# First self-attention of a decoder: second-half weight splits from GpSimd to ScalarE and VectorE, an own scratch for the normalised rows, the value bank emptied ahead of the inner norm's low parts, the decay prepared later

## Chip, core and metric

The kernel runs on one core of a Trainium2 chip. The metric is the device time in microseconds of one execution, the lower the better.

## The reference

Two decoder layers on x of 16 x 100 x 256, all in fp32. The change touches the first part only, layer 0's self-attention, which is a gated linear recurrence with a feed-forward part behind it:

```python
x = x + _L0_attn_ref(_layernorm(x), ...)      # then xattn, ffn, L1 attn, L1 xattn, L1 ffn

def _L0_attn_ref(x, ...):                     # B=16, L=100, 256 wide, H=16 heads of 64
    y = _layernorm(x) * ln1_g + ln1_b
    q, k, v = y @ Wq + bq, y @ Wk + bk, y @ Wv + bv      # each 256 -> 1024
    g = sigmoid(y @ Wg + bg)
    decay = sigmoid(decay_logit)[None, :, None]
    state = decay * state + k_t * v_t         # over the 100 steps
    out_t = g_t * q_t * state * DH ** -0.5
    x2 = x + out @ Wo + bo
    h = _layernorm(x2) * ln2_g + ln2_b
    return x2 + gelu(h @ W1 + b1) @ W2 + b2   # 256 -> 1024 -> 256
```

## The kernel before

The five engines have hand-written programs and wait for each other by counting semaphores; every order is the order of the code. An engine takes its instructions strictly in turn, so a wait holds all that stands behind it.

Rows go in 4 groups (NG) of 4 batch rows, 400 columns (N). The 1024 channels go in 8 blocks (KC) of 128. Block n of the whole stage is block n % 8 of group n // 8. TensorE's `project(n, kinds)` forms the four projections of a block, key, gate, value, query, each into a PSUM bank of its own (K_BANK0, G_BANK0, V_BANK0, Q_BANK0): only one block fits at a time, so a projection waits until the bank of the block before is emptied. ScalarE empties key and gate (`keys_gates`, into `kv` and `gate0`). VectorE empties value and query by multiplying them in (`gated`), and runs the recurrence (`scanned`: four scans and a product, into `state`). GpSimd splits the state (`heads_split`, into `oh0` and `ol0`), and TensorE sums it through Wo (`heads_summed`).

Each fp32 product is three matmuls on a high and a low part (fp32r): high is a cast, low the fp32 value less high. `split_matmul` (lines 764 to 766) does the three; the suffixes h and l name the parts (wk0h, wk0l, yTh, yTl, hTh, hTl, oh0, ol0; eh0 and el0 are the parts of the hidden values). The splits of weights and values are spread over ScalarE (casts), VectorE (`weights_low`) and GpSimd (`split`, lines 618 and 620). Before, the first column halves of Wk, Wg, Wv and Wq are split on ScalarE and VectorE, the second halves on GpSimd; Wo, W1 and W2 on ScalarE and VectorE.

At a group's end the steps are, on TensorE: the next group's first blocks (KC and KC+1, then keys and gates of KC+2) between the last head products, then the transposes of the inner norm's rows (`u0`, line 745), then value and query of KC+2, then `hidden` and `hidden_summed` (the feed-forward part). ScalarE writes the inner norm's rows to `full` and hTh, VectorE hTl from both, and both low parts (hTl of k = 0 and 1) are needed by the first hidden product. GpSimd's `hidden_split` splits the gelu's output from `full` into `eh0` and `el0`. Beside this VectorE rounds weights of a later layer (`blocks_rounded`, lines 2013 to 2019), and side jobs on TensorE transpose such weights; their results are parked in DRAM through the tile `parking`, which lies under `full`, `eh0` and `el0` in SBUF. Semaphore park_out counts these DMAs.

SP's queue loads x by groups and the weights, in the order of the code. ScalarE's queue loads the short vectors first, as rows of one tile, which TensorE turns into columns (`vec`, semaphore prep_vec; prep_done when ScalarE has copied them out).

## Time and profile before

| what | value |
|---|---|
| time, median of 3 runs | 1466.62 us (1465.25 to 1466.91) |
| the profiled execution: its own time | 1470.03 us |
| its span in the profile | 1468.2 us |
| granted TensorE clock over the span | 0.942 of full |
| TensorE busy | 1277.8 us, 87% |
| VectorE, ScalarE, GpSimd busy | 1043.7, 737.6, 256.4 us |

The table is read so: the span is from the first to the last instruction of one execution. The stage that is changed fills about the first 370 us of it. Busy times of engines overlap. A granted clock of 1 is 2.4 GHz, of 0.5 is 1.2 GHz.

### The profile page before, as it was taken

What the parts mean: (1) busy time and instruction counts of PE and PEld (TensorE: products, weight loads), DVE (VectorE), ACT (ScalarE), POOL (GpSimd) and SP (SyncE); (2) the same over time, 40 slices, a digit from 0 to 9 for tenths busy, and PEclk for the clock granted to TensorE, in tenths of its full rate; (3) what the DMA queues carried; (4) which work ended last, traced back from release to release, by engine and by line L of the source; (5) the groups of instructions that cost most, each with busy time, mean ns of one, the idle gap of its engine ahead of it and who ended that gap; (6) DMA issues with size and microseconds to landing.
All of it is one profiled execution on the core that took longest, in us unless ns stands there. A gap on an engine that the chain in (4) does not pass through costs nothing.

```text
span 1468.2 us, 27745 instructions
## 1 busy us (share of the span) xinstructions
PE 1277.8 (87%) x9826; PEld 1087.1 (74%) x9826; DVE 1043.7 (71%) x2592; ACT 737.6 (50%) x1808; POOL 256.4 (17%) x314
## 2 busy tenths in 40 slices
PE   4889888797899999999999999999879978969319
PEld 4878788796777777877778787877667756759318
DVE  5866466745567777777777777777589967885974
ACT  4442423325465555555655555565446643436473
POOL 3325252525100000000000000000044421000100
PEclk9899999998999999999999999999799989989759
DMA  9000101022100000000000000000020022300001
GB/s 282 31 22 1 44 1 44 1 77 80 35 11 11 12 1 11 10 11 10 11 11 10 1 10 11 10 1 1 1 58 2 3 66 62 100 7 1 0 0 46
DMA packets 34547, 40.66 MB, mean 28 GB/s; under 512 B 4889, under 2 KB 29066, under 8 KB 34442
## 3 DMA queue, kind: packets, MB, share of 16 engines
q1 hardware_dynamic: 33614, 39.24, 8.8%
q8 instruction: 51, 0.84, 0.2%
q14 instruction: 54, 0.44, 0.1%
q10 hardware_dynamic: 828, 0.14, 0.1%
HBM read 35.36 MB, written 4.01 MB: 27 GB/s over the span
## 4 chain that ended last, share of the span: by engine, by line
PE 51%; DVE 16%; issue 5%; ACT 4%; POOL 1%; DVEq 0%; ACTq 0%; POOLq 0%
PE bank L764 8%; PE bank L766 7%; PE bank L765 7%; PE bank L975 4%; PE bank L959 4%; PE bank L967 3%; PE bank L935 3%; ACT prob L1634 2%; DVE amax L2454 2%; DVE nmx L2270 2%; PE bank L1208 1%; PE bank L1226 1%; DVE kTl L2048 1%; PE bank L996 1%; PE bank L1293 1%
## 5 line engine op out<-in xcount | busy, mean ns | idle before, releaser
L1634 ACT ACTIVATE prob<-bank,nmx 100x361 f32<-100x361 f32 x256 | 142.7, 560 | 156.6 <-DVE nmx L2270 155.7
L2270 DVE TENSOR_REDUCE nmx<-bank 100x1 f32<-100x361 f32 x256 | 124.2, 526 | 22.8 <-PE bank L959 15.7
L690 POOL TENSOR_TENSOR frstd<-fmoments,eps 100x1 f32<-100x1 f32 x32 | 6.2, 193 | 648.5 <-DVE fmoments L2213 648.4
L764 PE MATMUL bank<-cxTh,wxkh 128*128 128x362 f32 x256 | 99.9, 390 | 2.8 <-DVE kTl L2048 2.8
L975 PEld LDWEIGHTS bank<-pT,vv 128*64 128x64 f32 (+1 forms) x1536 | 71.2, 139 | 37.5 <-issue 28.2
L975 PE MATMUL bank<-pT,vv 128*64 128x100 f32 (+1 forms) x1536 | 96.6, 261 | 1.9 <-DVE oTl L2047 1.8
L2287 DVE TENSOR_SCALAR prob<-prob,rsum 100x361 f32<-100x361 f32 x256 | 92.9, 405 | 4.5
L967 PE MATMUL bank<-ident,prob 100*128 100x100 f32 (+1 forms) x768 | 90.7, 254 | 1.5 <-DVE prob L2287 1.5
L967 PEld LDWEIGHTS bank<-ident,prob 100*128 100x128 f32 (+1 forms) x768 | 85.5, 153 | 7.1 <-DVE prob L2287 2.6
L2047 DVE TENSOR_TENSOR oTl<-bank,oTh 128x100 fp32r<-128x100 f32 x128 | 32.9, 257 | 81.2 <-ACT oTh L1620 78.0
L1620 ACT CAST oTh<-bank 128x100 fp32r<-128x100 f32 x128 | 31.8, 249 | 112.6 <-PE bank L975 112.4
L764 PE MATMUL bank<-wxvh,cxTh 128*128 128x512 f32 (+1 forms) x192 | 84.4, 440 | 2.8 <-DVE vv L2194 2.8
L765 PE MATMUL bank<-cxTl,wxkh 128*128 128x362 f32 x256 | 83.9, 328 | 0.0
L766 PE MATMUL bank<-cxTh,wxkl 128*128 128x362 f32 x256 | 83.9, 328 | 0.0
L2048 DVE SCALAR_TENSOR_TENSOR kTl<-bank,vec,kTh 128x362 fp32r<-128x362 f32 x128 | 75.2, 588 | 12.0 <-ACT kTh L1603 11.8
L1603 ACT ACTIVATE kTh<-bank,vec 128x362 fp32r<-128x362 f32 x128 | 72.3, 565 | 20.6 <-PE bank L766 20.2
L766 PE MATMUL bank<-wxvh,cxTl 128*128 128x512 f32 (+1 forms) x192 | 76.1, 396 | 0.0
L1985 DVE SCALAR_TENSOR_TENSOR kv<-bank,vec,kv 128x400 f32<-128x400 f32 x32 | 20.2, 632 | 78.1 <-PE bank L766 78.0
L765 PE MATMUL bank<-wxvl,cxTh 128*128 128x512 f32 (+1 forms) x192 | 75.4, 393 | 0.0
L935 PE MATMUL bank<-zT,wxq 128*128 (+1 forms) x256 | 58.9, 353 | 8.4 <-DVE oTl L2047 7.9
L715 POOL TENSOR_TENSOR s<-s,mx 100x400 f32<-100x400 f32 x64 | 54.2, 857 | 63.0 <-DVE mx L2349 61.2
L1626 ACT COPY pT<-bank 128x400 f32<-128x400 f32 x128 | 63.7, 498 | 1.6 <-PE bank L967 1.6
(403 smaller groups left out, 3794.8 us busy)
## 6 DMA issues: line engine op xcount, KB each, us to landing
cx<-in_ctx_dram SPq DMA_DIRECT2D x32, 128.0 KB, 2.1
xc<-in_ctx_dram SPq DMA_DIRECT2D x32, 128.0 KB
parked_weights<-parking SPq DMA_DIRECT2D x9, 256.0 KB, 5.6
mask_i<-in_mask_BxS_ik_dram SPq DMA_DIRECT2D x16, 141.0 KB
w<-in_L_attn_W_dram SPq DMA_DIRECT2D x2, 1024.0 KB, 13.6
cx<-in_ctx_dram SPq DMA_DIRECT2D x16, 105.0 KB, 2.1
xc<-in_ctx_dram SPq DMA_DIRECT2D x16, 105.0 KB
x<-in_x_dram SPq DMA_DIRECT2D x4, 400.0 KB
```

Source lines behind the costliest of these rows:

```text
L764: pe.matmul(o, wh, mh, start=start, stop=False)
L765: pe.matmul(o, wh, ml, start=False, stop=False)
L766: return pe.matmul(o, wl, mh, start=False, stop=stop)
L935: mm = pe.matmul(o[:, 0:2 * T], wxq[:, k, c * P:(c + 1) * P], zT[:, ds(pair_of_rows, 1), k, :].rearrange("d a q -> d (a q)"), start=(k == ...
L967: mm = pe.transpose(bank[T_BANKS[kt // 2]][0:r, col:col + T], prob[:, (2 * c + e) % 4, k0:k0 + r], ident[0:T, 0:T])
L975: mm = pe.matmul(bank[O_BANK][e * DH:(e + 1) * DH, 0:T], vv[0:r, kt, c * P + e * DH:c * P + (e + 1) * DH], pT[0:r, c % 2, kt, e * T:(e + 1 ...
L1603: nc.scalar.activation(kTh[:, c, :], src[:, 0:SP], ACT.Identity, bias=column("L0_xattn_bk", c)).then_inc(xa_kh, 1)
L1626: nc.scalar.copy(pT[:, c % 2, 0:2, :], bank[T_BANKS[0]][:, 0:4 * T].rearrange("p (k q) -> p k q", k=2))
L1634: nc.scalar.activation(prob[:, h % 4, :], bank[S_BANKS[e]][0:T, 0:S], ACT.Exp, bias=nmx[:, h:h + 1], accum_out=psum_[:, h:h + 1]).then_inc ...
L2048: return nc.vector.scalar_tensor_tensor(dst, src, bias, high.bitcast(F32), ALU.add, ALU.subtract)
L2270: nc.vector.tensor_reduce(nmx[:, h:h + 1], bank[S_BANKS[e]][0:T, 0:S], AX_X, ALU.max, negate=True).then_inc(xa_max, 1)
L2287: nc.vector.tensor_scalar(prob[:, h % 4, :], prob[:, h % 4, :], rsum[:, h:h + 1], None, ALU.mult).then_inc(xa_p, 1)
```

## The change

- The second halves of Wk, Wg, Wv and Wq are no longer split on GpSimd: ScalarE casts them in group 0 (keys and gates after block 1, values and queries after block 2), and VectorE takes the low parts behind block 1 and block 2. For that, statistics of x groups 1 to 3 move one block later on VectorE.
- SP loads Wo and the second halves ahead of the x groups 1 to 3.
- ScalarE writes the normalised rows to a new tile `y_rows`, not to `full`. So `rows_high0` no longer waits for hidden splits or for parking; the wait for parking now stands before the attention sums of groups 1 to 3.
- The decay's sigmoid goes behind the first weight casts, its transpose behind block 0 on TensorE, its copy behind block 0's key and gate on ScalarE; VectorE's first `gated` waits for it. The vectors are copied behind the first group's square roots.
- At a group's end VectorE empties and scans block KC+1 before hTl, and waits for GpSimd's first hidden split (l0_es) before the long additions and roundings.

```diff
@@ sync (SP)
                 load_half(name, dst, 0, wa_in[n])
+            load_raw("L0_attn_Wo", wo0[:], wo_in)
+            for name, dst in projections:
+                load_half(name, dst, 1, wb_in)
             for g in range(1, NG):
                 load_rows(g)
-            for name, dst in projections:
-                load_half(name, dst, 1, wb_in)
-            load_raw("L0_attn_Wo", wo0[:], wo_in)
@@ gpsimd
-                    nc.gpsimd.tensor_tensor(yTl[:, k, :], full[:, k, :], yTh[:, k, :].bitcast(F32), ALU.subtract).then_inc(l0_z, 1)
+                    nc.gpsimd.tensor_tensor(yTl[:, k, :], y_rows[:, k, :], yTh[:, k, :].bitcast(F32), ALU.subtract).then_inc(l0_z, 1)
             rows_low0(0)
-            pool.wait_ge(wb_in, 64)
-            for high, low, w in ((wk0h, wk0l, wk0), (wg0h, wg0l, wg0), (wv0h, wv0l, wv0), (wq0h, wq0l, wq0)):
-                split(high[:, :, 512:], low[:, :, 512:], w[:, :, 512:], l0_wb)
@@ tensor
-            pe.transpose(bank[SIDE_BANK0][:, 0:NV], rows[:], ident[0:NV, 0:NV])
-            pe.wait_ge(prep_decay, 1)
-            pe.transpose(bank[SIDE_BANK0][:, NV:NV + KC], decay_rows[:].rearrange("c h d -> c (h d)"), ident[0:KC, 0:KC])\
-                .then_inc(prep_vec, 1)
+            pe.transpose(bank[SIDE_BANK0][:, 0:NV], rows[:], ident[0:NV, 0:NV]).then_inc(prep_vec, 1)
...
                 project(c, range(4))
+                if c == 0:
+                    pe.wait_ge(prep_decay, 1)
+                    pe.transpose(bank[SIDE_BANK0][:, 0:KC], decay_rows[:].rearrange("c h d -> c (h d)"), ident[0:KC, 0:KC])\
+                        .then_inc(prep_vec, 1)
@@ scalar, rows_high0 and sums_out
-                if g:
-                    act.wait_ge(l0_es, KC * (g - 1))
-                if g > 1:
-                    act.wait_ge(park_out, 16 * 3 * (g - 1))
...
-                elif g == NG - 1:
+                elif g:
                     act.wait_ge(park_out, 16 * 3 * g)
@@ scalar, group 0
             first_deviations(1, 0, 1)
+            act.wait_ge(prep_vec, 1)
+            nc.scalar.mul(vecs[:], bank[SIDE_BANK0][:, 0:NV], DH ** -0.5)
+            nc.scalar.copy(vec[:], bank[SIDE_BANK0][:, 0:NV]).then_inc(prep_done, 1)
...
                     keys_gates(0)
+                    act.wait_ge(prep_vec, 2)
+                    nc.scalar.copy(decay[:], bank[SIDE_BANK0][:, 0:KC]).then_inc(prep_done, 1)
                     weights_high(wo_in, 16, wo0h, wo0, slice(0, D))
                     keys_gates(1)
+                    weights_high(wb_in, 64, wk0h, wk0, slice(512, C))
+                    weights_high(wb_in, 64, wg0h, wg0, slice(512, C))
                 for c in range(2, KC):
                     if c > 2 or g == 0:
                         keys_gates(first + c)
+                    if g == 0 and c == 2:
+                        weights_high(wb_in, 64, wv0h, wv0, slice(512, C))
+                        weights_high(wb_in, 64, wq0h, wq0, slice(512, C))
@@ vector, group 0
-            dve.wait_ge(prep_done, 1)
+            dve.wait_ge(prep_done, 2)
...
                 if g == 0:
-                    first_stats(1)
                     gated(0)
                     scanned(0)
                     weights_low(4, wo0l, wo0, wo0h, slice(0, D))
                     gated(1)
                     scanned(1)
+                    weights_low(5, wk0l, wk0, wk0h, slice(512, C), l0_wb)
+                    weights_low(6, wg0l, wg0, wg0h, slice(512, C), l0_wb)
...
                         if c == 2:
+                            weights_low(7, wv0l, wv0, wv0h, slice(512, C), l0_wb)
+                            weights_low(8, wq0l, wq0, wq0h, slice(512, C), l0_wb)
+                            first_stats(1)
+                        if c == 3:
                             first_stats(2)
-                        if c == 3:
                             first_stats(3)
@@ vector, group end
+                if follows:
+                    gated(first + KC + 1)
+                    scanned(first + KC + 1)
                 for k in range(KD):
                     dve.wait_ge(l0_hh, KD * g + k + 1)
                     nc.vector.tensor_tensor(hTl[:, k, :], full[:, k, :], hTh[:, k, :].bitcast(F32), ALU.subtract).then_inc(l0_h, 1)
                 if follows:
-                    gated(first + KC + 1)
-                    scanned(first + KC + 1)
                     gated(first + KC + 2)
                     scanned(first + KC + 2)
+                    dve.wait_ge(l0_es, first + 1)
```

VectorE in group 0, from block 1's value and query on. Names are tiles, `kv<-bank` empties the value bank. Before:

```order
L1985 SCALAR_TENSOR_TENSOR kv<-bank,vec,kv 128x400
L1989 SCALAR_TENSOR_TENSOR gate<-bank,vec,gate 128x400
L2000 SCALAR_TENSOR_TENSOR state<-decay,kv 128x100 x4
L2004 SCALAR_TENSOR_TENSOR state<-gate,state 128x400
L1985 SCALAR_TENSOR_TENSOR kv<-bank,vec,kv 128x400
L1989 SCALAR_TENSOR_TENSOR gate<-bank,vec,gate 128x400
L2000 SCALAR_TENSOR_TENSOR state<-decay,kv 128x100 x4
L2004 SCALAR_TENSOR_TENSOR state<-gate,state 128x400
L1931 MEMSET pause 1x1
L1933 BN_STATS stats_all<-x 100x6 x4
```

And now:

```order
L1987 SCALAR_TENSOR_TENSOR kv<-bank,vec,kv 128x400
L1991 SCALAR_TENSOR_TENSOR gate<-bank,vec,gate 128x400
L2002 SCALAR_TENSOR_TENSOR state<-decay,kv 128x100 x4
L2006 SCALAR_TENSOR_TENSOR state<-gate,state 128x400
L1980 TENSOR_TENSOR wk0l<-wk,wk0h 128x2x512
L1980 TENSOR_TENSOR wg0l<-wg,wg0h 128x2x512
L1987 SCALAR_TENSOR_TENSOR kv<-bank,vec,kv 128x400
L1991 SCALAR_TENSOR_TENSOR gate<-bank,vec,gate 128x400
L2002 SCALAR_TENSOR_TENSOR state<-decay,kv 128x100 x4
L2006 SCALAR_TENSOR_TENSOR state<-gate,state 128x400
L1980 TENSOR_TENSOR wv0l<-wv,wv0h 128x2x512
L1980 TENSOR_TENSOR wq0l<-wq,wq0h 128x2x512
```

Four low parts have come in (L1980), two behind block 1 and two behind block 2, and the statistics of x (BN_STATS) stand behind them. What GpSimd had there (its rows now begin with oh) is gone from its queue.

VectorE at the first group's end, from the inner norm's rows on. Before:

```order
L1864 TENSOR_SCALAR u<-zg,moments,rstd 100x256 x4
L2150 TENSOR_TENSOR hTl<-full,hTh 128x400 x2
L1985 SCALAR_TENSOR_TENSOR kv<-bank,vec,kv 128x400
L1989 SCALAR_TENSOR_TENSOR gate<-bank,vec,gate 128x400
L2000 SCALAR_TENSOR_TENSOR state<-decay,kv 128x100 x4
L2004 SCALAR_TENSOR_TENSOR state<-gate,state 128x400
L1985 SCALAR_TENSOR_TENSOR kv<-bank,vec,kv 128x400
L1989 SCALAR_TENSOR_TENSOR gate<-bank,vec,gate 128x400
L2000 SCALAR_TENSOR_TENSOR state<-decay,kv 128x100 x4
L2004 SCALAR_TENSOR_TENSOR state<-gate,state 128x400
L2157 TENSOR_TENSOR x<-x,zg 100x1024
```

And now:

```order
L1866 TENSOR_SCALAR u<-zg,moments,rstd 100x256 x4
L1987 SCALAR_TENSOR_TENSOR kv<-bank,vec,kv 128x400
L1991 SCALAR_TENSOR_TENSOR gate<-bank,vec,gate 128x400
L2002 SCALAR_TENSOR_TENSOR state<-decay,kv 128x100 x4
L2006 SCALAR_TENSOR_TENSOR state<-gate,state 128x400
L2159 TENSOR_TENSOR hTl<-full,hTh 128x400 x2
L1987 SCALAR_TENSOR_TENSOR kv<-bank,vec,kv 128x400
L1991 SCALAR_TENSOR_TENSOR gate<-bank,vec,gate 128x400
L2002 SCALAR_TENSOR_TENSOR state<-decay,kv 128x100 x4
L2006 SCALAR_TENSOR_TENSOR state<-gate,state 128x400
L2165 TENSOR_TENSOR x<-x,zg 100x1024
```

One block's value, query and scans (kv to state) have moved ahead of the low parts hTl. The addition to x (last row) now waits for GpSimd's first hidden split.

ScalarE from the square roots to block 1's key. Before:

```order
L1434 ACT_TABLE_LOAD
L1434 ACTIVATE decay_rows<-logits 8x128
L1437 COPY decay<-bank 128x8
L1438 ACTIVATE vecs<-bank 128x80
L1439 COPY vec<-bank 128x80
L1455 ACT_TABLE_LOAD
L1455 ACTIVATE std_all<-first_moments,eps 100x4
L1457 ACTIVATE std_all<-var_z,eps 100x4
L1512 CAST wk0h<-wk 128x2x512
L1512 CAST wg0h<-wg 128x2x512
L1468 ACTIVATE full<-bank,vec 128x400
L1469 ACTIVATE yTh<-bank,vec 128x400
```

And now:

```order
L1449 ACT_TABLE_LOAD
L1449 ACTIVATE std_all<-first_moments,eps 100x4
L1451 ACTIVATE std_all<-var_z,eps 100x4
L1511 ACTIVATE vecs<-bank 128x80
L1512 COPY vec<-bank 128x80
L1502 CAST wk0h<-wk 128x2x512
L1502 CAST wg0h<-wg 128x2x512
L1458 ACTIVATE y_rows<-bank,vec 128x400
L1459 ACTIVATE yTh<-bank,vec 128x400
L1458 ACTIVATE y_rows<-bank,vec 128x400
L1459 ACTIVATE yTh<-bank,vec 128x400
L1502 CAST wv0h<-wv 128x2x512
```

The sigmoid of the decay and its table load are gone from the head, and y_rows takes the place of full.

## Rows read from the trace of the kernel before

**Rows 1.** The page, busy times of the engines.

```profile
PE 1277.8 (87%) x9826; PEld 1087.1 (74%) x9826; DVE 1043.7 (71%) x2592; ACT 737.6 (50%) x1808; POOL 256.4 (17%) x314
```

**Rows 2.** TensorE's waits, 0 to 450 us: total, times, longest.

```profile
PE bank L764 <- DVE kv L1985: 20.0, 5, 7.2
PE bank L764 <- POOL yTl L639: 11.7, 4, 3.9
...
PE bank L764 <- POOL el L620: 10.7, 16, 1.7
```

**Rows 3.** Windows after six waits: busy of five engines, granted clock (0.50), DMA, GB/s.

```profile
42.22:47.38 5.16, 5.16 (x15) 5.16 (x16) 3.76 (x9) 0.00 (x0) 2.45 (x3) 0.50 0.01 3
101.76:105.40 3.64, 3.64 (x11) 3.60 (x12) 2.74 (x7) 0.10 (x1) 1.35 (x2) 0.53 0.00 0
164.07:170.24 6.17, 6.17 (x18) 6.11 (x19) 0.00 (x0) 1.78 (x3) 1.45 (x2) 0.50 0.00 0
184.95:190.78 5.83, 5.83 (x18) 5.78 (x19) 4.09 (x12) 0.09 (x1) 1.56 (x2) 0.50 0.00 0
248.55:252.20 3.65, 3.65 (x11) 3.61 (x12) 0.00 (x0) 0.59 (x1) 1.44 (x2) 0.53 0.00 0
268.19:272.69 4.50, 4.50 (x13) 4.46 (x14) 2.76 (x8) 0.10 (x1) 1.56 (x2) 0.50 0.00 0
```

**Rows 4.** Timelines of ScalarE and TensorE, the start: start, length, instruction.

```profile
8.83 1.28 ACT L1434 ACT_TABLE_LOAD   x1 [8.83 <-issue]
...
13.55 0.30 ACT L1455 ACTIVATE std_all<-first_moments,eps 100x4 f32<-100x4 f32 x1
...
21.26 0.70 PE L764 MATMUL bank<-yTh,wk0h 128*128 128x400 f32 x1 [2.95 <-POOL yTl L639]
```

**Rows 5.** Timeline of VectorE, group 0.

```profile
29.12 6.90 DVE L2000 TENSOR_TENSOR_SCAN state<-decay,kv 128x100 f32<-128x100 f32 x4
...
37.20 4.42 DVE L1978 TENSOR_TENSOR wo0l<-wo,wo0h 128x2048 fp32r<-128x2048 f32 x1
...
53.90 1.12 DVE L2000 TENSOR_TENSOR_SCAN state<-decay,kv 128x100 f32<-128x100 f32 x4
...
57.83 2.25 DVE L1978 TENSOR_TENSOR w1l<-w,w1h 128x2048 fp32r<-128x2048 f32 x1
```

**Rows 6.** Timeline of GpSimd, first and last of its second-half splits (8 instructions).

```profile
25.31 1.04 POOL L618 CAST wk0h<-wk 128x1024 fp32r<-128x1024 f32 x1 [4.10 <-DMA wq<-in_L_attn_Wq_dram]
...
36.93 2.55 POOL L620 TENSOR_TENSOR wq0l<-wq,wq0h 128x1024 fp32r<-128x1024 f32 x1
```

**Rows 7.** Timelines: TensorE and ScalarE, rows of groups 1 and 2.

```profile
83.65 0.45 PE L764 MATMUL bank<-yTh,wk0h 128*128 128x400 f32 x1 [1.29 <-POOL yTl L639]
...
160.51 0.68 ACT L1468 ACTIVATE full<-bank,vec 128x400 f32<-128x400 f32 x1 [4.73 <-DMA parked_weights<-parking]
```

**Rows 8.** SP's timeline and the DMA list (last column: us to landing).

```profile
22.36 3.98 SPq L509 DMA_DIRECT2D raw<-in_L_attn_W_attn_dram  x1
...
raw<-in_L_attn_W_attn_dram SPq DMA_DIRECT2D x1, 768.0 KB, 13.5
```

**Rows 9.** Timelines at the first group's end: VectorE, TensorE, GpSimd.

```profile
100.59 0.57 DVE L2150 TENSOR_TENSOR hTl<-full,hTh 128x400 fp32r<-128x400 f32 x1 [0.57 <-ACT hTh L1566]
...
131.27 0.63 DVE L1985 SCALAR_TENSOR_TENSOR kv<-bank,vec,kv 128x400 f32<-128x400 f32 x1 [8.83 <-PE bank L766]
...
101.76 0.51 PE L764 MATMUL bank<-yTh,wv0h 128*128 128x400 f32 x1 [4.05 <-DVE kv L1985]
...
108.62 1.88 POOL L620 TENSOR_TENSOR el<-full,eh 128x400 fp32r<-128x400 f32 x1
...
120.91 2.42 POOL L620 TENSOR_TENSOR el<-full,eh 128x400 fp32r<-128x400 f32 x1
...
123.87 1.05 POOL L620 TENSOR_TENSOR el<-full,eh 128x400 fp32r<-128x400 f32 x1
```

More of the change, by code:

```diff
@@ L205, in decoder_kernel @@
             el0 = sb("el0", [P, 2, N], F32R, scope=s)
+            y_rows = sb("y_rows", [P, KD, N], scope=s)
         with ExitStack() as s:
@@ L771, in side_job @@
                 o = bank[SIDE_BANK0 + j % 2]
+                if j == 0:
+                    pe.wait_ge(prep_done, 2)
                 if raw is not None:
@@ L1431, in _ @@
             act.dma_start(rel[0:BUCKETS, :], a["L1_attn_rel_emb"]).then_inc(small_in, 16)
-            act.wait_ge(vec_in, 16 * VEC_DMAS)
-            nc.scalar.activation(decay_rows[:], logits[:].unsqueeze(2).broadcast_to([KC, 2, DH]), ACT.Sigmoid)\
-                .then_inc(prep_decay, 1)
-            act.wait_ge(prep_vec, 1)
-            nc.scalar.copy(decay[:], bank[SIDE_BANK0][:, NV:NV + KC])
-            nc.scalar.mul(vecs[:], bank[SIDE_BANK0][:, 0:NV], DH ** -0.5)
-            nc.scalar.copy(vec[:], bank[SIDE_BANK0][:, 0:NV]).then_inc(prep_done, 1)
             act.wait_ge(memsets, 2)
@@ L1467, in rows_high0 @@
                     src, scale, bias = bank[SIDE_BANK0 + k][:, 0:N], column("L0_attn_ln1_g", k), column("L0_attn_ln1_b", k)
-                    nc.scalar.activation(full[:, k, :], src, ACT.Identity, scale=scale, bias=bias)
+                    nc.scalar.activation(y_rows[:, k, :], src, ACT.Identity, scale=scale, bias=bias)
                     nc.scalar.activation(yTh[:, k, :], src, ACT.Identity, scale=scale, bias=bias).then_inc(l0_y, 1)
@@ L1524, in _ @@
             weights_high(wa_in[3], 16, wq0h, wq0, slice(0, 512))
+            nc.scalar.activation(decay_rows[:], logits[:].unsqueeze(2).broadcast_to([KC, 2, DH]), ACT.Sigmoid)\
+                .then_inc(prep_decay, 1)
             for g in range(NG):
@@ L1973, in rows_once_normalized, with weights_low @@
                 link(ins)
-            def weights_low(n, low, w, high, cols):
+            def weights_low(n, low, w, high, cols, done=l0_wl):
                 dve.wait_ge(l0_wh, n + 1)
-                nc.vector.tensor_tensor(low[:, :, cols], w[:, :, cols], high[:, :, cols].bitcast(F32), ALU.subtract).then_inc(l0_wl, 1)
+                nc.vector.tensor_tensor(low[:, :, cols], w[:, :, cols], high[:, :, cols].bitcast(F32), ALU.subtract).then_inc(done, 1)
             def gated(n):
@@ L2108, in _ @@
                         if c == 2:
+                            weights_low(7, wv0l, wv0, wv0h, slice(512, C), l0_wb)
+                            weights_low(8, wq0l, wq0, wq0h, slice(512, C), l0_wb)
+                            first_stats(1)
+                        if c == 3:
                             first_stats(2)
-                        if c == 3:
                             first_stats(3)
                             first_variances(1, NG)
-                            weights_low(5, w1l, w1, w1h, slice(0, C))
+                            weights_low(9, w1l, w1, w1h, slice(0, C))
                         if c == 4:
                             second_variances(3, 1, NG)
-                            weights_low(6, w2l, w2, w2h, slice(0, D))
+                            weights_low(10, w2l, w2, w2h, slice(0, D))
                             both_deviations(3, 1, NG)
```

## Prediction

> **What bounds the kernel now.** I read the page's first part, then the list of TensorE's waits, then the timelines of the engines around each long wait. TensorE is busy 87% of the span [rows 1]; it is the engine to keep fed. Over the first 450 us, where all edits lie, its list of waits has three lines that this change can touch [rows 2]: 20.0 us for the value bank (line 1985 on VectorE empties it), 11.7 us for the low parts of the rows (yTl), 10.7 us for the low parts of the hidden values (el). Nothing after about 370 us is edited, so what is saved before should arrive at the end unchanged: nothing there runs at a fixed time.
>
> A wait costs more than its length. After the six longest waits the granted clock is 0.50 to 0.53, that is 1.2 instead of 2.4 GHz, for 3.6 to 6.2 us each [rows 3]; at full clock the same matmuls need about half, so each window costs half its length: 2.6, 1.8, 3.1, 2.9, 1.8 and 2.3 us. A wait of 1.29 [rows 7] and those for el, none longer than 1.7 [rows 2], have no such window behind them.
>
> **The change part by part.**
>
> Head start. ScalarE begins with the sigmoid's table at 8.83 and only reaches the square root at 13.55; TensorE's first projection starts at 21.26, behind a chain of root, rows, transposes and splits [rows 4]. With the sigmoid gone, the table loaded at 8.83 is the root's, so the root starts at 8.83+1.28 = 10.11 and the whole chain 3.4 us earlier: **3.4 us**. The copies of the vectors go behind the two roots and end near 12, before the rows are ready (13.3).
>
> Stall in the first group. GpSimd splits the second halves from 25.31 to 39.5 (36.93+2.55) [rows 6]. Beside it VectorE's four scans take 6.90 us where 1.12 is usual, and the split of Wo 4.42 where one of the same size takes 2.25 [rows 5]. So the value bank of the second column block (block 1) is emptied only when TensorE has waited 7.2 us for it, until 42.22 [rows 2, 3]. With those splits off GpSimd, VectorE comes to that block 5.8+2.2 = 8 us earlier. Wait 7.2 and slow window 2.6 go: **9.8 us**.
>
> What it costs there. VectorE gets four subtractions, each half of the 2.25 one [rows 5]: some 4.6 us; ScalarE gets four casts, which I put at 1 us each (GpSimd's took 1.04 [rows 6]). I laid the engines out. At half clock a matmul takes 5.16/15 = 0.34 [rows 3], at full clock then 0.17 to 0.18, and the four projections of a block (24 matmuls) 4.3; block 0 starts at 17.8, mostly at half clock, and ends near 24.8. ScalarE: decay copy 25.4, Wo's cast to 27.3, then the halves at 28.5 and 32.2. VectorE must wait for the decay (25.4 instead of 24.0) and behind the scan and Wo's low part empties block 1's value bank near 32, needed at 31.6 (wait 0.5); the raw weights for the first side transposes land at 22.36+13.5 = 35.9 [rows 8], which nothing in the change hastens, while TensorE is there at 35.4 (0.5); the statistics of groups 2 and 3 and W1's low parts now stand behind a VectorE that is already late, so block 4's value bank is emptied near 54.8 against 51.9 needed (2.9). Three losses of 1 us on VectorE beside GpSimd's splits of the state are in this. Without them the wait of 2.9 is nearly gone; with whole splits (1.6 us) lost instead, it is about 5. I take **-4** in all, bounds -1 and -6.5.
>
> A rule speaks here. Beside GpSimd's work the scans, which read decay and kv from SBUF, took six times their usual time, and Wo's low part twice [rows 5]. So who comes second may lose a whole instruction of the other. "SBUF — State Buffer" of the Trainium skill (Who interferes with whom) says that a VectorE instruction with two SBUF inputs and a GpSimd one that reads SBUF exclude each other for the whole instruction. The trace agrees for these two. By that rule the moved subtractions, with two such inputs, would lose whole instructions too: the -4 would then be -6.5 and the time 1433.
>
> Rows' own scratch. Before groups 2 and 3 ScalarE waits for the parking DMAs (4.73 us, until 160.51) because `full` lies under them [rows 7]. With y_rows it doesn't. In group 1's turn, which has no such wait, TensorE still waits 1.29 [rows 7]. So the waits before groups 2 and 3, which are the rest of the 11.7 after 2.95 and 1.29 [rows 2, 4, 7], 7.4 together, become 1.3 each: 4.8, and two windows (3.1+1.8) go: **9.7 us**. The wait for parking moves to the attention sums on ScalarE. Between the old wait's end and these stand the rows' evictions and low parts (3.5 us), two projections (2.2) and a head product (1.1), 6.8 us, and the rows now come 2.6 earlier: still 4 us behind the DMA. Landing 4 us later, it would be seen.
>
> Value bank before the low parts. At each of three boundaries TensorE waits 4.0 us for the value bank (4.05, 3.99, 3.99; the 20.0 less 7.2 and a small 0.7) [rows 2, 9]. VectorE is then idle till ScalarE's high parts are there. Its inputs (the next group's block 1: value and query) were projected before the keys and gates of block 2, which TensorE has just finished, so it empties the bank at 97.4; TensorE, free at 97.7, goes on at once. The scan ends at 99.6, before the second high part releases the low one (100.59, ends 101.2) [rows 9]. Then the value and query projections take 2.2 us, and the hidden product waits for the low parts: 101.2-99.9 = 1.3, and about 1.45 in the other two. Gain 12.0 - 4.2 = 7.8, and the windows 1.8+2.9+2.3 = 7.0 go: **14.8 us**. If VectorE's scan ran slowly there, only the 1.3 would grow.
>
> The new wait on the first hidden split. VectorE now starts its long additions and roundings after GpSimd's first el. Before, that subtraction took 1.88 where 1.05 is usual [rows 9], and TensorE's longest wait for el was 1.7 [rows 2]. Three times some 1.1 us: +3.2. But the roundings then begin about 2.5 us later against TensorE and meet the last splits, with no slack behind. Nothing before shows that order: bounds +3.2 and -5; I take **+2**. VectorE itself has 8.83 us idle behind the roundings [rows 9], so its lateness alone costs nothing.
>
> First statistics later and x loaded later: groups 1 to 3 of x are needed after 43 now, and are loaded ahead of W1 and of the raw weights, in by 35.9: nothing.
>
> **Sum.** 3.4+9.8-4+9.7+14.8+2 = 35.7 us. The profiled execution took 1470.03 around its span of 1468.2, so this one would take 1434.3 with a span of 1432.5; the median of the three runs is 1466.62, so 1430.9, say 1431. Own range, 1426 to 1437.
>
> **The rivals.**
> - *VectorE becomes the bound in group 0.* It works nearly without a pause from 25 to 60 already in my layout. If its low parts lose time beside GpSimd as Wo's did (2.2 us each), the bank waits grow by 4 to 6, and the wait of 2.9 becomes as long as those with a slow window behind: gain 29, 1437. 14%.
> - *The roundings lock out the last hidden splits.* The low part (line 620) took 2.42 instead of 1.05 where it met them before, at 120.91 [rows 9], in the sixth split, with two uncontended ones behind. If seventh and eighth meet them, each group loses 1.4+1.4, and the +2 becomes 3.2-8.4 = -5: gain 29, 1438. 9%.
> - *The wait only moves at the boundary.* If the low parts come 2 us later than I think, the wait before the hidden product is as long as those that have a slow window behind them now [rows 3]: 3 x (2+2): gain 24, 1443. 5%.
> - *Nearly none of the new waits.* The -4 is -1, the splits +3: gain 40, 1427 or a little less. 8%.
> - *Slower.* Wo and the second halves share one queue and ScalarE waits for all four halves with block 2's key eviction behind it. They landed at 25.3 [rows 6], are needed at 28.5; each us beyond is a us of TensorE. They would have to land after 28.5+36 = 64 to end slower. The raw weights behind them in the queue were in by 35.9 [rows 8], so 2%.
> The forecast itself: 62%.
>
> **Numbers.** 1424 to 1442 holds the forecast and the first two rivals whole, and leaves out the third, the slower one and a bit of the fourth; it is wide because the contention has no row for the new order. A difference within 0.2% (3 us) can't be told from none: no case lies there but a mishap, 1%; slower 2%; faster 97%.
>
> **What the profile after would show.** First projection near 17.8; no value wait of 7 us near 35, scans of 1.1 us throughout group 0; casts of second halves on ScalarE before 35; row evictions of groups 2 and 3 without a DMA wait; at the boundaries the value projection straight behind the transposes, and a wait of 1.3 to 1.5 for hTl at full clock; the first el at 1.05. Wrong would be: a long wait for kv in group 0 with the clock at half behind it, hTl after 102 (in old time), or el of splits 6 to 8 above 2 us in every group.

## The result and the profile after

The changed kernel takes 1442.83 us (median of 4 runs, 1441.94 to 1443.37), the kernel before beside it 1466.59 (1465.25 to 1466.91): ratio 0.984, 95% interval 0.9825 to 0.9854. It is 23.8 us faster; 35.7 were forecast, and 1442.83 lies just above the range of 1424 to 1442. The profiled execution took 1443.37 with a span of 1441.2, 27.0 less than before.

The page's busy times answer to [rows 1], TensorE's waits up to 450 us (total, times, longest) to [rows 2]:

```profile
PE 1271.4 (88%) x9826; PEld 1080.2 (75%) x9826; DVE 1044.2 (72%) x2596; ACT 740.2 (51%) x1811; POOL 249.8 (17%) x306
```

```profile
PE bank L759 <- DVE hTl L2159: 8.7, 4, 2.4
PE bank L759 <- POOL el L621: 8.7, 8, 2.3
PE bank L759 <- POOL yTl L640: 6.7, 4, 2.9
...
PE bank L759 <- DVE kv L1987: 1.4, 2, 0.7
PE bank L786 <- DMA raw<-in_L_attn_W_attn_dram: 1.0, 1, 1.0
```

The value bank's 20.0 us are down to 1.4, those for yTl from 11.7 to 6.7 as worked out. But hTl, 2.4 before (one wait, in the last group), stands at 8.7, and el has lost only 2.0 while its longest wait grew from 1.7 to 2.3. The windows behind the new waits (columns as in [rows 3]: stretch, length, busy of five engines, granted clock, DMA, GB/s):

```profile
92.01:95.14 3.13, 3.13 (x9) 3.10 (x10) 2.56 (x7) 0.59 (x1) 0.03 (x1) 0.50 0.00 0
112.02:115.50 3.48, 3.48 (x11) 3.43 (x12) 0.00 (x0) 0.00 (x0) 1.44 (x2) 0.55 0.02 5
187.08:190.50 3.42, 3.42 (x11) 3.37 (x12) 0.00 (x0) 0.00 (x0) 1.45 (x2) 0.56 0.02 5
244.06:248.00 3.94, 3.94 (x15) 3.92 (x16) 3.00 (x7) 1.19 (x2) 1.77 (x3) 0.68 0.00 0
167.87:171.00 3.13, 3.13 (x17) 3.13 (x18) 3.01 (x7) 1.19 (x2) 0.96 (x2) 1.00 0.00 0
```

The first four stretches have half clock in them: the first from its start, the next two from 0.4 us on (9 to 11 matmuls in 3.1 to 3.5 us), the fourth only from 1.4 us on (0.68 in the mean). The last one, at full clock, holds 17 matmuls in 3.13. By this count half clock costs about 1.5 us each time; priced as in the prediction, at half of the time spent at half clock, it is 1.7, the figure used below.

The chain at the start (ScalarE, TensorE; [rows 4]), then VectorE and GpSimd in the first group ([rows 5, 6]):

```profile
8.84 1.28 ACT L1449 ACT_TABLE_LOAD   x1 [8.84 <-issue]
10.14 0.30 ACT L1449 ACTIVATE std_all<-first_moments,eps 100x4 f32<-100x4 f32 x1
...
17.85 0.70 PE L759 MATMUL bank<-yTh,wk0h 128*128 128x400 f32 x1 [2.95 <-POOL yTl L640]
```

```profile
28.24 2.29 DVE L1980 TENSOR_TENSOR wo0l<-wo,wo0h 128x2048 fp32r<-128x2048 f32 x1
...
31.53 1.50 DVE L2002 TENSOR_TENSOR_SCAN state<-decay,kv 128x100 f32<-128x100 f32 x4
...
33.56 1.22 DVE L1980 TENSOR_TENSOR wk0l<-wk,wk0h 128x1024 fp32r<-128x1024 f32 x1
34.70 1.54 DVE L1980 TENSOR_TENSOR wg0l<-wg,wg0h 128x1024 fp32r<-128x1024 f32 x1
```

```profile
28.39 2.51 POOL L619 CAST oh<-state 128x400 fp32r<-128x400 f32 x1 [10.59 <-DVE state L2006]
```

The start gained 3.41 (3.4 forecast). Scans and low parts now run at or near their usual length. It is GpSimd's cast (usually 0.52) that takes 2.51 beside Wo's low part, and nobody waits for it.

The first group's end, VectorE, GpSimd and TensorE, which answers to [rows 9]:

```profile
87.73 1.13 DVE L2002 TENSOR_TENSOR_SCAN state<-decay,kv 128x100 f32<-128x100 f32 x4
88.89 0.57 DVE L2006 SCALAR_TENSOR_TENSOR state<-gate,state 128x400 f32<-128x400 f32 x1
89.38 0.57 DVE L2159 TENSOR_TENSOR hTl<-full,hTh 128x400 fp32r<-128x400 f32 x1
90.50 1.37 DVE L2159 TENSOR_TENSOR hTl<-full,hTh 128x400 fp32r<-128x400 f32 x1 [0.54 <-ACT hTh L1568]
```

```profile
89.53 0.80 POOL L619 CAST oh<-state 128x400 fp32r<-128x400 f32 x1 [6.12 <-DVE state L2006]
90.41 1.02 POOL L621 TENSOR_TENSOR ol<-state,oh 128x400 fp32r<-128x400 f32 x1
```

```profile
92.01 0.67 PE L759 MATMUL bank<-hTh,w1h 128*128 128x400 f32 x1 [2.12 <-DVE hTl L2159]
```

The state that VectorE now finishes at 89.5 releases GpSimd's split of it (oh, ol), and this split lies right on hTl: the second part, begun 0.09 behind ol, takes 1.37 where 0.57 is usual, and TensorE waits 2.12, not 1.3.

And the roundings, VectorE, GpSimd, TensorE:

```profile
96.78 1.51 DVE L2165 TENSOR_TENSOR x<-x,zg 100x1024 f32<-100x1024 f32 x1 [2.18 <-POOL el L621]
...
109.13 1.95 DVE L2021 TENSOR_TENSOR raw<-raw,blk_scale 128x1536 f32<-128x1536 f32 x1
```

```profile
95.71 1.05 POOL L621 TENSOR_TENSOR el<-full,eh 128x400 fp32r<-128x400 f32 x1
...
97.29 1.91 POOL L621 TENSOR_TENSOR el<-full,eh 128x400 fp32r<-128x400 f32 x1
...
109.55 2.42 POOL L621 TENSOR_TENSOR el<-full,eh 128x400 fp32r<-128x400 f32 x1
```

```profile
112.02 0.45 PE L759 MATMUL bank<-eh,w2h 128*128 128x400 f32 x1 [2.34 <-POOL el L621]
```

VectorE waits 2.18 us for the first el, which is 1.05 long now; the next one takes the 1.91 instead. The rounding's last multiplication begins at 109.13 and meets the seventh split, whose subtraction takes 2.42.

Checkpoints of TensorE in both profiles; a gain is the start before less the start after, a step is what a stage adds to it:

| start of | before | after | gain | step | forecast |
|---|---|---|---|---|---|
| first projection | 21.26 | 17.85 | 3.41 | 3.4 | 3.4 |
| projection of group 1 | 83.65 | 73.62 | 10.03 | 6.6 | 5.8 |
| hidden, group 0 | 105.60 | 92.01 | 13.59 | 3.6 | 4.55 |
| key of block 11 on ScalarE | 129.03 | 117.16 | 11.87 | -1.7 | +0.7 |
| projection of group 2 | 164.07 | 149.57 | 14.50 | 2.6 | 2.5 |
| hidden, group 1 | 189.12 | 167.87 | 21.25 | 6.75 | 8.55 |
| key of block 19 on ScalarE | 212.85 | 192.21 | 20.64 | -0.6 | +0.7 |
| projection of group 3 | 248.55 | 225.70 | 22.85 | 2.2 | 2.3 |
| hidden, group 2 | 272.36 | 244.06 | 28.30 | 5.45 | 6.65 |
| key of block 27 on ScalarE | 295.80 | 267.88 | 27.92 | -0.4 | +0.7 |
| end | 1468.2 | 1441.2 | 27.0 | -0.9 | 0 |

The forecast column is made of the prediction's terms, cut at these points. "Hidden" is the first hidden product of a group, so the half clock behind the wait for hTl counts in the step after it. The three boundaries (the steps up to "hidden") lack 4.0 us, the three hidden phases (the steps up to "key of block") 4.8, the end 0.9; the first group gave 0.8 more.

### The profile page after: what moved, and what is told of

It is laid out like the page before. It is cut to its first block, busy times and chain, and to the rows that moved or that the text cites. A ratio compares the mean times of both kernels' runs of the same rounds, so it can differ in the third digit from the quotient of the medians.

```text
span 1441.2 us, 27742 instructions
## 1 busy us (share of the span) xinstructions
PE 1271.4 (88%) x9826; PEld 1080.2 (75%) x9826; DVE 1044.2 (72%) x2596; ACT 740.2 (51%) x1811; POOL 249.8 (17%) x306
## 4 chain that ended last, share of the span: by engine, by line
PE 51%; DVE 17%; issue 5%; ACT 4%; POOL 1%; DVEq 0%; ACTq 0%; POOLq 0%
PE bank L759 8%; PE bank L761 7%; PE bank L760 7%; PE bank L976 4%; PE bank L960 4%; PE bank L968 3%; PE bank L936 3%; ACT prob L1636 2%; DVE amax L2462 2%; DVE nmx L2278 2%; PE bank L1209 1%; PE bank L1227 1%; DVE kTl L2050 1%; PE bank L997 1%; PE bank L1241 1%
## 5 line engine op out<-in xcount | busy, mean ns | idle before, releaser
L1605 ACT ACTIVATE kTh<-bank,vec 128x362 fp32r<-128x362 f32 x128 | 72.2, 564 | 20.9 <-PE bank L761 20.5
```

The lines of the kernel that those rows point to most:

```text
L1605: nc.scalar.activation(kTh[:, c, :], src[:, 0:SP], ACT.Identity, bias=column("L0_xattn_bk", c)).then_inc(xa_kh, 1)
```

## The experiments

The kernel before was timed again beside these kernels: 1467.54 us beside the first four below, 1468.54 beside c_both, c_both_no_wait, b_group0 and b_bank_first, 1468.03 beside the other four. So they are compared with the change by their ratios to it, and by their medians; a thousandth is 1.5 us, and the change stands at 0.984 (0.9825 to 0.9854).

**a_no_wait: the changed kernel without the new wait.**

```diff
                     scanned(first + KC + 2)
-                    dve.wait_ge(l0_es, first + 1)
```

> The changed kernel without VectorE's wait for GpSimd's first hidden split. Theory A (the wait shifts the roundings onto the seventh split): the roundings start 2.2 us earlier, the first el takes 1.9 instead of 1.05, the seventh 1.05 to 1.7 instead of 2.42; TensorE's waits for el stay under 1.8 and the half clock behind the seventh goes in the two groups that have it. Gain (1.3 + 1.7) x 2 + 0.5, less 0.9 x 3: about 4 us, 1439. Rival B (the wait brings what I had put on it, +2, and the loss lies elsewhere): 1445. Within 1 us of 1443 would say that both sides cancel.

Measured: 1443.32 us, ratio 0.9838 (0.9824 to 0.9852), no different from the change. In the first group the first two el are at 1.04 and 1.06, the last multiplication comes at 106.51 and falls on a cast, and no wait for el is above 0.7. In the second and third group it falls on a subtraction again (2.42 both times); the third:

```profile
259.37 1.95 DVE L2021 TENSOR_TENSOR raw<-raw,blk_scale 128x1536 f32<-128x1536 f32 x1
```

```profile
262.26 0.45 PE L759 MATMUL bank<-eh,w2h 128*128 128x400 f32 x1 [2.32 <-POOL el L621]
```

TensorE waits 8.5 us for el against 8.7, and half clock follows the wait of 2.32. So the new wait is worth nothing that can be told from noise: neither A nor B. Without it VectorE loses its time to the splits in other places; what decides is which split the last multiplication meets.

**a_lows_first: the old order at the boundary.**

```diff
-                if follows:
-                    gated(first + KC + 1)
-                    scanned(first + KC + 1)
                 for k in range(KD):
                     dve.wait_ge(l0_hh, KD * g + k + 1)
...
                 if follows:
+                    gated(first + KC + 1)
+                    scanned(first + KC + 1)
```

> The changed kernel with hTl ahead of the scan of block KC+1 again at each group end; all else as changed. Theory A: the order of the boundary brought most of what I forecast for it (14.8) less 0.8 x 3 of a slower hTl and some 3.4 of half clock: it costs 9 to 11 us to undo, 1452 to 1454, with waits of 4.0 for kv at three boundaries and half clock behind them. Rival B (the order brought nearly nothing, the slow hTl ate it): 1444 to 1447. Rival C (the full 14.8, the shortfall is elsewhere): 1458.

Measured: 1455.53 us, ratio 0.9917 (0.9899 to 0.9935): (0.9917 - 0.984) x 1467 = 11.3 us above the change by the ratios, with some 3.5 of uncertainty, and 12.7 by the medians. The waits for kv are back (12.8 in 4, longest 4.1), with half clock behind each of the three at the boundaries. That is A's 9 to 11 or a little more. C, the full 14.8, lies at the edge of that uncertainty.

**a_scan_split: the state's product behind hTl.**

```diff
                 if follows:
                     gated(first + KC + 1)
-                    scanned(first + KC + 1)
+                    scans(first + KC + 1)
                 for k in range(KD):
...
                 if follows:
+                    weighed(first + KC + 1)
                     gated(first + KC + 2)
```

(`scans` is the four scans, `weighed` the product with gate0.)

> The changed kernel with only the product with the gate (which lets GpSimd split the state) moved behind both hTl; the bank is emptied and the four scans run ahead of hTl as in the change. Theory A (GpSimd's split of that state slows the second hTl): hTl takes 0.57 instead of 1.37, TensorE's wait before the hidden product 1.3 instead of 2.1 in all three groups, and if a wait of 1.3 has no half clock behind it, two windows of 1.7 go too: 2.4 + 3.4 = 6 us, 1437. Without the windows 1440.5. Rival B (hTl is slow for another reason, ScalarE's reads of PSUM or the write to hTh beside it): hTl stays at 1.37 and the time at 1443.

Measured: 1442.80 us, ratio 0.9843 (0.9827 to 0.9858): no gain. The mechanism at the boundary is as A had it, VectorE, GpSimd, TensorE:

```profile
90.35 0.57 DVE L2168 TENSOR_TENSOR hTl<-full,hTh 128x400 fp32r<-128x400 f32 x1 [0.51 <-ACT hTh L1568]
```

```profile
91.47 0.52 POOL L619 CAST oh<-state 128x400 fp32r<-128x400 f32 x1 [8.19 <-DVE state L2010]
```

```profile
91.07 0.42 PE L759 MATMUL bank<-hTh,w1h 128*128 128x400 f32 x1 [1.38 <-DVE hTl L2168]
...
108.39 0.45 PE L759 MATMUL bank<-eh,w2h 128*128 128x400 f32 x1 [1.20 <-POOL el L621]
...
112.08 0.70 PE L759 MATMUL bank<-eh,w2h 128*128 128x400 f32 x1 [2.33 <-POOL el L621]
```

All six hTl take 0.57 to 0.58, the wait is 1.3 to 1.4 in all three groups, at full clock. That the split of the state was what slowed hTl is shown. But the roundings end when they did (109.19 + 1.95), so TensorE and the splits, a us earlier, meet them one split later: TensorE waits 1.20 more for the seventh split, and 2.33 with half clock for the eighth, on which the last multiplication now falls, in all three groups: el 12.8 us against 8.7. What the boundary gave, the roundings took. (The expectation for c_both below calls these the sixth and seventh split; counted in the trace they are the seventh and eighth.)

**a_round_late: the last multiplication behind the eighth split.**

```diff
                 link(nc.vector.tensor_scalar(flat, flat, 7.0, -8.0, ALU.min, ALU.max))
+                dve.wait_ge(l0_es, splits)
                 nc.vector.tensor_tensor(blocks(flat), blocks(flat), over(blk_scale[:], n), ALU.mult).then_inc(prep_q, 1)
```

(`splits` is first + KC, all of the group's hidden splits.)

> The changed kernel with the last multiplication of the block rounding (1.95 us, two operands from SBUF) held until the group's eighth hidden split is done. Theory A: el of the seventh split 1.05 instead of 2.42, TensorE's wait for it (2.34, 2.34, 1.74) falls by 1.3 each, and the half clock behind it in two groups (1.7 each) goes: 3.9 + 3.4 = 7 us, 1436. VectorE then ends near 115.6 and is next needed at 119.4, so its lateness costs nothing. Rival B (the seventh split is slow from the clock or from PSUM, or the next split takes the wait over): 1441 to 1443.

Measured: 1436.27 us, ratio 0.9786 (0.9769 to 0.9803), 6.6 us faster than the change by the medians, 7.9 by the ratios: A. GpSimd, VectorE, TensorE:

```profile
110.32 1.02 POOL L621 TENSOR_TENSOR el<-full,eh 128x400 fp32r<-128x400 f32 x1
```

```profile
113.04 1.76 DVE L2022 TENSOR_TENSOR raw<-raw,blk_scale 128x1536 f32<-128x1536 f32 x1 [3.17 <-POOL el L621]
117.69 0.63 DVE L1987 SCALAR_TENSOR_TENSOR kv<-bank,vec,kv 128x400 f32<-128x400 f32 x1 [2.89 <-PE bank L761]
```

```profile
111.40 0.45 PE L759 MATMUL bank<-eh,w2h 128*128 128x400 f32 x1 [0.94 <-POOL el L621]
```

The seventh split takes 1.02 instead of 2.42, the longest wait for el is 0.9 and no half clock stands behind one (in the first three groups only behind one wait for hTl, 2.07, and the one for the raw weights). VectorE still has 2.89 us idle behind it. This was so although this execution waited 3.24 us for the raw weights in group 0, with 1.7 of half clock, against 0.98 in the change's.

**The parts alone, on the kernel before.** Each diff is the matching piece of the change and nothing else.

*b_group0: head, second halves, loads, statistics and decay.*

> The kernel before with the first group's part of the change alone (head, second-half splits off GpSimd, order of loads, statistics, decay); rows in the old scratch, old order at the group ends, no new wait. By my terms 3.4 + 9.8 - 4 = 9.2 us off, 1457 to 1458; by the trace of the changed kernel 10.3, and 12 if the roundings and later windows fall well. Rival (part of the gain of the first group needs the other parts): 1460 or more.

Measured: 1459.70 us, ratio 0.9934 (0.9917 to 0.9951), 8.8 less than before beside it and 0.3 short of the rival's 1460; by the ratio it is 9.7. Group 1's projection starts at 73.56, as in the change (73.62), so this stage did not need the other parts.

*b_bank_first: value bank and scan ahead of hTl, without the new wait.*

> The kernel before with block KC+1's value bank emptied and scanned ahead of hTl, and nothing else. By my term 14.8 off: 1452. By the changed kernel's trace the slow hTl (0.8 x 3) and half clock behind hTl remain: 9 to 12 off, 1455 to 1458, as undoing it in the changed kernel cost 12.7. Rival (what it frees is taken back by the waits for the parked rows in groups 2 and 3 and by el): 1460 or more.

Measured: 1458.90 us, ratio 0.9929 (0.9910 to 0.9948), 9.6 less, far from my term of 14.8 and 0.9 above the 1455 to 1458 expected from the changed kernel's trace. Its hTl is slow too (1.34 at 98.85, wait 2.20 with half clock behind it), but its waits for el are no longer than 1.6. Its first group is the code of before, and there TensorE waited 5.67 for the value bank where before's profile has 7.24. From the first projection to that of group 1 it took 60.8 us (21.09 to 81.91), before's profiled execution 62.4 (21.26 to 83.65), and b_rows_only, with the same order in this group, 61.3 (22.71 to 83.98): before's was the slowest of the three, by 1.1 to 1.6 us.

*b_rows_only: y_rows.*

> The kernel before with the rows' own scratch alone. By my term 9.7 off: 1458. By the changed kernel's trace the two waits for the parked rows go to 1.3 (2.6 and 2.2 saved) with their half clock (3.1 and 1.8, of which the clock list shows 1.7 each): 8.2 off, 1459.5. Rival (part of it goes into the next long wait for kv, which stands right behind in both groups): 1462 or more.

Measured: 1460.02 us, ratio 0.9945 (0.9928 to 0.9962), 8.0 less. The waits for yTl in front of groups 2 and 3 fall to 1.25 and 1.23; the waits for kv that follow them are 3.99 and 4.05, as they were, so nothing of the gain went there.

The three gains add up to 28 us by the ratios, with some 4 to 5 of uncertainty, and to 26.4 by the medians, against 23.8 for the change. That they take from each other, because an earlier TensorE meets the same roundings, would fit a_scan_split, but the difference is not clear of the noise.

**c_both: both orders together** (a_scan_split and a_round_late).

> The changed kernel with both orders: the state's product behind hTl, and the last multiplication of the block rounding behind the eighth hidden split. Theory A (the product's order gave 0.8 us a boundary, which the last multiplication took back at the sixth and seventh split): against the order of the rounding alone (1436.3) it now keeps 2.3 us, and the half clock behind hTl that one group still had (1.7): 1432 to 1433. Rival B (what is gained at the boundary is always taken back by the multiplication in the middle, which isn't moved): 1435 to 1437.

Measured: 1436.80 us, ratio 0.9781 (0.9767 to 0.9795), as a_round_late alone. The time is B's, but not for B's reason: the multiplication in the middle did not take the gain back. TensorE waits 1.20 and 0.94 for el in each group, and still its trace keeps a gain for 200 us: at the last group's head sums (before 329.24) it is at 293.25, a_round_late at 295.70. Then it loses the 2.4 again: 8.5 us of clock go between 294 and 311 where a_round_late loses 6.8, and from the cross-attention's first product to the end it takes 1100.3 against 1099.2 us, in code that is the same.

**c_both_no_wait: the same without the new wait.**

> As the kernel with both orders, but also without VectorE's wait for the first hidden split. The additions and roundings start up to 2.5 us earlier, so the multiplication in the middle meets the fourth or fifth split and not the fifth or sixth. Theory A (the wait of the change is worth nothing, only moves which split is slow): within 1.5 us of the kernel with both, 1431 to 1434. Rival B (it is worth its +2): 1434.5 or more.

Measured: 1437.28 us, ratio 0.9787 (0.9774 to 0.9801). The time is in B's range only because c_both itself was 4 us above what A took for it; against c_both the difference is 0.5, so the new wait is worth nothing here that can be seen in the time. The traces differ more. Both have the same two waits for el, 1.2 and 0.94, close together in each group; behind them the clock stays full in c_both (first line) and falls in c_both_no_wait in two groups of three (second line):

```profile
111.92:115.60 3.68, 3.68 (x20) 3.68 (x21) 1.76 (x1) 1.19 (x2) 0.00 (x0) 1.00 0.00 0
110.68:114.00 3.32, 3.32 (x12) 3.32 (x11) 1.43 (x1) 0.00 (x0) 0.00 (x0) 0.50 0.00 0
```

In return its wait of 2.17 for the raw weights has no half clock behind it, where c_both's 2.93 has.

**a_eh_scalar: ScalarE writes the high part of the hidden values.**

```diff
-                split(eh0[:, n % 2, :], el0[:, n % 2, :], full[:, n % 2, :], l0_es)
+                nc.gpsimd.tensor_tensor(el0[:, n % 2, :], full[:, n % 2, :], eh0[:, n % 2, :].bitcast(F32), ALU.subtract)\
+                    .then_inc(l0_es, 1)
...
-                    nc.scalar.activation(full[:, c % 2, :], bank[SIDE_BANK0 + c % 2][:, 0:N], ACT.Gelu,
-                                         bias=column("L0_attn_b1", c)).then_inc(l0_gelu, 1)
+                    src = bank[SIDE_BANK0 + c % 2][:, 0:N]
+                    nc.scalar.activation(full[:, c % 2, :], src, ACT.Gelu, bias=column("L0_attn_b1", c))
+                    if n == 0:
+                        act.wait_ge(line_in, 16)
+                    if n > 1:
+                        act.wait_ge(l0_w2, KD * (n - 1))
+                    nc.scalar.activation(eh0[:, c % 2, :], src, ACT.Gelu, bias=column("L0_attn_b1", c)).then_inc(l0_gelu, 1)
```

> The changed kernel with the high part of the hidden values written by ScalarE (the same gelu once more, 0.59 us) and GpSimd left with the subtraction only: 1.05 to 2.4 a block where it has 1.6 to 3.7. Theory A (what TensorE waits for is GpSimd's row of splits, pushed by the roundings): waits for el nearly gone, 8.7 us to 2 or less, with the half clock behind the seventh split: some 6.5 + 3.4 = 10 us off, 1433; hTl is still slow. Rival B (TensorE's pace of 2.2 us a block is near ScalarE's now, and the second gelu delays the first split by 0.6): 1438 or more.

Measured: 1439.58 us, ratio 0.9808 (0.9793 to 0.9822), 3.3 us faster by the medians, 4.7 by the ratios, less than half of what A said. GpSimd now stands idle between the subtractions, but that does not help it past the multiplication:

```profile
106.43 1.05 POOL L635 TENSOR_TENSOR el<-full,eh 128x400 fp32r<-128x400 f32 x1 [0.75 <-ACT eh L1583]
108.59 2.39 POOL L635 TENSOR_TENSOR el<-full,eh 128x400 fp32r<-128x400 f32 x1 [1.10 <-ACT eh L1583]
```

It stands idle 1.10 us and is then held all the same by the multiplication at 108.34; TensorE waits 2.06 in two groups, with half clock behind both. So the row of splits was a part of the wait, and the single collision, which a_round_late takes away for 6.6 to 7.9, the larger one.

**c_raw: c_both, raw weights ahead of W1 and W2 in SP's queue.**

> The kernel with both orders, and the first raw weights (for TensorE's first side transposes) loaded ahead of W1 and W2. In the profile of the kernel with both orders TensorE waits 2.93 us for that DMA, with 1.7 of half clock behind it; in the changed kernel 0.98. Theory A: the wait goes in every execution: 1 to 4.6 us off, 1432 to 1435.5, and a narrower spread. Rival B (W1 and W2 land later and stop ScalarE's casts, or the value banks of group 0 wait in its place): 1436 or more.

Measured: 1437.55 us, ratio 0.9787 (0.9770 to 0.9805): no gain, B. The wait for the DMA is gone, and two blocks later TensorE waits for VectorE:

```profile
52.06 0.45 PE L759 MATMUL bank<-yTh,wv0h 128*128 128x400 f32 x1 [1.87 <-DVE kv L1987]
```

This is the 2.9 of my layout of block 4. In the change the DMA's wait had given VectorE time to catch up (0.70 there).

**c_all: c_raw with ScalarE's high parts.**

> As the kernel with both orders and the early raw weights, with the high part of the hidden values on ScalarE. Theory A: the two waits for el that are left in a group (1.20 and 0.94) go: 3 x 2.1 = 6.4 us off that kernel, about 1428. Rival B (ScalarE is the new bound in the hidden phase): no gain over it, 1433 or more.

Measured: 1430.69 us (1428.93 to 1432.05), ratio 0.9744 (0.9730 to 0.9757) against 1468.03 of before beside it. It is the fastest here, 12 us below the change by the medians, 14 by the ratios, and 6.9 (medians) or 6.3 (ratios) below c_raw, as A had it (6.4); 1428 was not reached, because c_raw came out higher than A took it. TensorE's waits up to 450 us, and two of its windows:

```profile
PE bank L760 <- POOL yTl L641: 6.7, 4, 2.9
PE bank L760 <- DVE hTl L2175: 6.3, 4, 2.4
...
PE bank L760 <- POOL el L635: 2.7, 6, 0.7
PE bank L760 <- DVE kv L1993: 2.6, 2, 1.9
```

```profile
91.05:95.00 3.95, 3.85 (x19) 3.29 (x20) 3.92 (x8) 2.77 (x6) 2.93 (x4) 1.00 0.00 0
108.76:112.50 3.74, 3.74 (x21) 3.74 (x22) 1.76 (x1) 1.24 (x2) 0.00 (x0) 1.00 0.00 0
```

From 28 to 291 us the granted clock is full throughout. ScalarE was not the new bound (B).

## Why the prediction was right and wrong

Two steps of the prediction failed, the boundary's and the new wait's; the other three terms held within 1.7 us.

*Head start, 3.4:* right, 3.41.

*Stall in the first group, 9.8, less 4:* right within a us. The stage gave 6.6 of 5.8; alone with the head it is 8.8 timed (9.2 forecast). Some of that is luck: the stall that went was 1.1 to 1.6 us larger in before's profiled execution than in the two others with this order. Of the new losses, the wait of 0.98 for the raw weights and 0.70 for block 4's value bank stand where I had 0.5 and 2.9: they are one loss, that c_raw moves from the one to the other (1.87). By "SBUF — State Buffer" (Trainium skill, Who interferes with whom), such a VectorE instruction and a GpSimd one that reads SBUF exclude each other, and the order in which they are issued decides which of them is blocked. I had reckoned that by it the moved subtractions would lose whole instructions, and the -4 would be -6.5. The trace agrees with the rule and not with that use of it: GpSimd's cast began 0.15 behind Wo's low part and took 2.51 instead of 0.52, while two of the four moved subtractions began first (33.56 and 38.90, 1.22 long) and the other two lost 0.3 behind a cast (34.70 and 40.03, 1.54).

*Rows' own scratch, 9.7:* right in mechanism. The waits fell to 1.26 and 1.23, the DMA was not seen at the attention sums, alone it is 8.0 timed. Part of the difference is the price of the windows: in b_rows_only the stretches behind the two waits, to the next wait for the value bank, got 2.8 and 1.5 us shorter (18.0 for 20.9, 18.1 for 19.6), where half their length had given 3.1 and 1.8.

*Value bank before the low parts, 14.8:* the order was right, its size was not: 11.3 by a_lows_first, 9.6 alone. The step that failed is "The scan ends at 99.6, before the second high part releases the low one ... 101.2-99.9 = 1.3": I asked what VectorE does at that time and not what the state it finishes sets free. GpSimd's split of that state fell on the low part, and the wait was 2.12, 2.02 and 2.06 for the 1.3, 1.45 and 1.45 forecast; a_scan_split shows this, where the split comes later and hTl takes 0.57 again. That is 2.0 of the 4.0 us that the boundaries lack. The rest lies in part in the price of the windows, as for the rows; no run settles it. Half clock stood behind two of the three waits as well, and counts in the hidden phases.

*The new wait, +2:* the other step that failed. I had seen that the roundings "meet the last splits, with no slack behind" and still took a gain of 2. The new wait itself is worth nothing: 1443.32 us without it and 1442.83 with it. The hidden phases lost 2.7 in place of gaining 2. They hold the half clock behind two waits for hTl, and the last multiplication on the seventh split, where TensorE waits 2.34, 2.34 and 1.74 with half clock behind two; moving that one instruction gave 6.6 to 7.9. My rival "the roundings lock out the last hidden splits" had this mechanism, at 1.4 + 1.4 a group and without the clock, and 9%. Of my signs of being wrong, the one for this (el of splits 6 to 8 above 2 us in every group) nearly came: the seventh split has a subtraction of 2.42 in two groups and a cast of 2.04 in the third.

*The number of another rival came true by luck.* "The wait only moves at the boundary" has a gain of 24 and 1443. It wanted low parts that come 2 us late with half clock behind all three; they came 0.6 to 0.8 late with half clock behind two, and the rest of the shortfall lies in the hidden phases.

*A short wait has no window.* This assumption failed under both: behind the start, my rows had waits of 1.7 or less and of 3.6 or more, nothing between. The trace of before did hold one, in the last group, that my rows left out. Its wait of 1.96 has half clock behind it, from 1.5 us on, before the next long wait begins at 332.8:

```profile
329.24 0.45 PE L764 MATMUL bank<-oh,wo0h 128*128 128x400 f32 x1 [1.96 <-POOL ol L620]
330.70:332.80 2.10, 1.91 (x8) 1.49 (x8) 0.69 (x1) 2.07 (x4) 0.00 (x0) 0.50 1.00 400
```

Here waits of 2.0 to 2.3 are followed by half clock more often than not, and each such window costs about 1.7.

*Profiled execution and median.* Before's profiled execution lay 3.4 above its median, after's 0.5. The sum was made against one and moved to the other unchanged. Some 1.1 to 1.6 of the 3.4 may lie in the very stall that the change removes (b_bank_first, b_rows_only); two other executions are not a median, so this is an estimate.

The 8.7 us by which the spans differ from the sum are thus 4.0 + 4.8 + 0.9 - 0.8 (8.9, since the forecast column adds up to 35.85). What makes the last 0.9, behind all edits, I can't say beyond this: the same code there takes 1097.7 us in before's profile, 1098.7 in after's and 1100.3 in c_both's.

## What to carry to other kernels

When an instruction is moved forward, list what its semaphore releases and where that lands: here a split on another engine, on the one instruction that TensorE waited for. Where two engines hinder each other, look for the single long instruction that meets the short ones TensorE waits for. Hold it until the last short one is through, if its own engine has idle time behind: here this gave 6.6 us or more for one added wait, more than making all the short ones shorter did (3.3 to 4.7, a_eh_scalar). And a gain in front of a fixed train of work can be lost to that train, as in a_scan_split: look for the next thing that TensorE meets when it is 1 us early.

## What the runs showed of the hardware that I had not expected

- Waits of TensorE of 1.2 to 1.4 us had full clock behind them, but for one trace: in c_both_no_wait two pairs of waits (1.21 and 0.94, then 1.20 and 0.94) had half clock behind them, where the same pairs in c_both and c_raw had none. Of the waits of 2.0 to 2.2 (for hTl and el, groups 0 to 2), ten of seventeen had half clock behind them: in the change 2.12 and 2.06 had it and 2.02 not, in a_round_late 2.07 and not 2.16 or 2.03. All nine of 2.32 to 2.34 for el (the change, a_scan_split, a_lows_first, a_no_wait) had it. So the length of a wait alone did not decide it here. The stretch at 1.2 GHz cost about 1.5 to 1.7 each time.
- When GpSimd's split and a two-input VectorE instruction met, either could lose, and in the change's three cases it was the one that began second: hTl 1.37 for 0.57 (90.50, behind ol at 90.41), el 2.42 for 1.05 (109.55, behind the multiplication at 109.13), oh 2.51 for 0.52 (28.39, behind wo0l at 28.24, which kept its usual 2.29).
- The first block runs slowly in every trace: in the change's, 6 matmuls start in the 2.15 us from 17.85 (0.33 apart, the pace of the stretches at half clock) and 17 in the 3.00 us from 25, though the granted clock is given as 1.00 in both. How long this lasts varies: about 8 matmuls at that pace in a_round_late and c_both, about 16 in the change.
- The landing of the first raw weights, behind all of this stage's weights in the same queue, varied between executions of nearly the same program: TensorE was released at 36.05 in the change's profile and at 37.08 in a_round_late's.
